# Moving the steps of a time-mixing stage: next scan ahead of the quotient, and a new order for the last of eight batches

## What is computed

```
x = x + _L1_attn_ref(_layernorm(x), ...)          # time mixing, this stage
x = x + _L1_ffn_ref(_layernorm(x), ...)           # its router logits are made in this stage too

k, v = xk @ Wk.T, xv @ Wv.T ; r = sigmoid(xr @ Wr.T)
step: qt = max(pp, kt + u); e1 = exp(pp - qt); e2 = exp(kt + u - qt)
      out = (e1 * aa + e2 * vt) / (e1 * bb + e2)
      pp_new = max(pp + neg_ew, kt); f1 = exp(pp - pp_new); f2 = exp(kt - pp_new)
      aa, bb = f1 * aa + f2 * vt, f1 * bb + f2
ln = layernorm(wkv) * ln_g + ln_b ; result = (r * ln) @ Wo.T
```

## Time and profile before

| What | us |
|---|---|
| median of 3 executions | 732.92 (732.75 to 733.7) |
| the profiled execution, its own time | 731.65 |
| its span in the profile | 729.7 |
| busy in the span: PE / DVE / ACT / POOL | 660.3 / 518.9 / 349.0 / 337.1 |
| the stage of the change: first load of its products to its last matmul | 403 to 564 |

### The profile page before, as it was taken

How to read it: one execution, slowest core, us unless ns; L and a number is a source line. 1 busy time by engine, 2 the same in 40 slices (tenths; PEclk the granted TensorE clock), 3 DMA queues, 4 the chain that set the end, 5 groups by cost and what they waited for, 6 DMA issues and landing times. The chain is left out here.

```text
span 729.7 us, 13761 instructions
## 1 busy us (share of the span) xinstructions
PE 660.3 (90%) x4339; PEld 538.6 (74%) x4339; DVE 518.9 (71%) x1087; ACT 349.0 (48%) x735; POOL 337.1 (46%) x326
## 2 busy tenths in 40 slices
PE   8989999879989999999997999999988679999950
PEld 6656666568868888888886888888877348888840
DVE  5878888957865555544444699998782868888847
ACT  1767777736403333333333565554552844554420
POOL 4977767510053344334224255555331066777530
PEclk9999999998999999999999999999976799999985
DMA  6900000101013111111106940000010022333229
GB/s 197 337 2 3 1 2 15 45 11 53 1 56 105 58 59 51 52 58 55 34 22 206 363 146 2 1 0 1 30 58 30 1 65 76 101 101 102 78 81 311
DMA packets 37185, 54.23 MB, mean 74 GB/s; under 512 B 6644, under 2 KB 28918, under 8 KB 36982
## 3 DMA queue, kind: packets, MB, share of 16 engines
q1 hardware_dynamic: 27832, 31.78, 13.0%
q0 software_dynamic: 7104, 19.41, 8.5%
q10 hardware_dynamic: 2176, 2.10, 0.9%
HBM read 37.28 MB, written 15.99 MB: 73 GB/s over the span
## 5 line engine op out<-in xcount | busy, mean ns | idle before, releaser
L1926 PE MATMUL banks<-r_xt,r_w_mixed 128*128 128x256 f32 x384 | 84.9, 380 | 0.7 <-ACT r_xt L2023 0.7
L1577 DVE SCALAR_TENSOR_TENSOR f0x_s<-f0x_th,banks 128x512 f32<-128x512 f32 x35 | 24.1, 687 | 83.2 <-ACT f0x_th L1536 83.2
L1437 POOL DMA_INDIRECT f_y<-f0x_yout,f_slot_of x35 | 34.5, 984 | 99.6 <-ACT f0x_yout L1552 99.6
L1926 PEld LDWEIGHTS banks<-r_xt,r_w_mixed 128*128 128x128 f32 x384 | 72.1, 189 | 11.0 <-ACT r_xt L2023 1.0
L1536 ACT ACTIVATE f0x_th<-banks 128x512 f32<-128x512 f32 x35 | 21.0, 600 | 86.9 <-PE banks L1488 86.9
L1423 POOL DMA_INDIRECT f0x_xg<-f_xn,f_token_of x35 | 34.9, 996 | 55.7 <-DVE f_slot_of L1046 44.3
L659 DVE TENSOR_REDUCE a_ssum<-a_e 128x6 f32<-128x1536 f32 x32 | 56.0, 1748 | 1.3 <-ACT a_e L526 1.0
L1488 PE MATMUL banks<-f_w_hi,f0x_xt_hi 128*128 x140 | 55.4, 396 | 0.9 <-DVE f0x_xt_lo L1571 0.9
L1488 PE MATMUL banks<-f_w_lo,f0x_xt_hi 128*128 x140 | 55.6, 397 | 0.0
L1423 POOL DMA_INDIRECT f1x_xg<-f_xn,f_token_of x39 | 40.6, 1041 | 32.4 <-DVE f_slot_of L1046 19.3
L1488 PE MATMUL banks<-f_w_hi,f0x_xt_lo 128*128 x140 | 55.2, 394 | 0.0
(11 more groups left out here) (368 smaller groups left out, 1895.9 us busy)
## 6 DMA issues: line engine op xcount, KB each, us to landing
f_w_lo<-in_f_w13T SPq DMA_DIRECT2D x4, 2048.0 KB, 11.1
r_y<-f_y SPq DMA_DIRECT2D x16, 256.0 KB, 4.9
f_w_lo<-in_f_w2T SPq DMA_DIRECT2D x4, 512.0 KB, 15.1
f_xn<-f_rows_normed SPq DMA_DIRECT2D x8, 256.0 KB, 2.1
f_b<-in_f_b SPq DMA_DIRECT2D x1, 2048.0 KB, 10.1
f_w_lo<-in_f_w2T SPq DMA_DIRECT2D x2, 1024.0 KB, 11.9
f_xn<-r_y SPq DMA_DIRECT2D x8, 256.0 KB
f1c_y<-f_y SPq DMA_DIRECT2D x8, 256.0 KB, 7.8
```

Of the source, the lines that this page charges most:

```text
L1437: pool.indirect_dma_start(k.y_dram, bass.IndirectOffsetOnAxis(ap=k.slot_of[:, done:done + 1], axis=0), yout[:, done % YB, :], None).then_i ...
L1577: dve.scalar_tensor_tensor(out=s1[:, t % 2, :], in0=th[:, t % 2, :], scalar=1.0, in1=glu_part, op0=ALU.add, op1=ALU.mult).then_inc(s1_done, 1)
L1926: last = pe.matmul(bank(1 + kind)[:, eb * T:(eb + 1) * T], r.w_mixed[:, kind, j // KB, j % KB, eb * P:(eb + 1) * P], xt[:, b % 2, j % KB, ...
```

## The change

In the loop, `tops(b)` no longer stands in iteration b ahead of `gate(b-1)`, but in iteration b-1, behind the reciprocal and ahead of the multiplication into `r_wkv`, which is now a step of its own (`quotient`). `falls(b)` moves ahead of `gate(b-1)`. `divide` as a step of POOL is unchanged.

After the loop, `shift(7)` moves from behind `centre(7)` to between the router chunks, two matmuls on unused data are added on PE (`keep_clock(2)`, four records), `late_turn(4)` and `late_turn(5)` go between centre and project, `deviate(7)` moves ahead of `project(7)`, and on ACT `late_norm(5)` goes behind `late_turn(3)` and `late_norm(6)` further back.

```
         w.stats(2)
         for z in range(LATE):
             w.shared_add(z)
-        IN_GAP = 4
         for b in range(B):
             if b + 1 < B:
                 front(b + 1)
             if b > 0:
                 w.centre(b - 1)
-            w.tops(b)
+            if b == 0:
+                w.tops(b)
+            w.falls(b)
             if b > 0:
                 w.square(b - 1)
                 w.gate(b - 1)
                 w.shift(b - 1)
-            w.falls(b)
             w.grow(b)
             w.gap(b)
             w.clamp(b)
@@ -1797,6 +1797,9 @@
             if b > 0:
                 w.vary(b - 1)
             w.divide(b)
+            if b + 1 < B:
+                w.tops(b + 1)
+            w.quotient(b)
             if b + 3 < B:
                 w.gather_up(b + 3)
             if b > 0:
@@ -1804,27 +1807,39 @@
             if B - 3 <= b < B - 1:
                 w.late_norm(2 * (b - B + 3))
                 w.late_norm(2 * (b - B + 3) + 1)
+        last = B - 1
         w.late_turn(0)
-        for c in range(IN_GAP):
-            if c + 1 < IN_GAP:
-                w.late_turn(c + 1)
-            if c < 2:
-                w.late_norm(4 + c)
-            w.late_gates(c)
-        w.level(B - 2)
-        for step in (w.centre, w.square, w.gate, w.shift, w.add_shift, w.project, w.deviate, w.vary):
-            step(B - 1)
-        w.late_norm(B - 2)
-        w.late_turn(IN_GAP)
-        for c in range(IN_GAP, B - 1):
-            if c + 1 < B - 1:
-                w.late_turn(c + 1)
-            w.late_gates(c)
-        w.add(B - 1)
-        w.level(B - 1)
-        w.late_norm(B - 1)
-        w.late_turn(B - 1)
-        w.late_gates(B - 1)
+        w.late_turn(1)
+        w.late_gates(0)
+        w.late_turn(2)
+        w.late_norm(4)
+        w.late_gates(1)
+        w.late_turn(3)
+        w.shift(last)
+        w.late_gates(2)
+        w.late_gates(3)
+        w.late_norm(5)
+        w.keep_clock(2)
+        w.centre(last)
+        w.level(last - 1)
+        w.square(last)
+        w.late_turn(4)
+        w.gate(last)
+        w.deviate(last)
+        w.late_turn(5)
+        w.project(last)
+        w.add_shift(last)
+        w.vary(last)
+        w.late_gates(4)
+        w.late_norm(6)
+        w.late_gates(5)
+        w.late_turn(6)
+        w.late_gates(6)
+        w.add(last)
+        w.level(last)
+        w.late_norm(last)
+        w.late_turn(last)
+        w.late_gates(last)
 
     class Work:
         def shared_up(self, z): pass
@@ -1847,6 +1862,8 @@
         def clamp(self, b): pass
         def scan(self, b): pass
         def divide(self, b): pass
+        def quotient(self, b): pass
+        def keep_clock(self, times): pass
         def centre(self, b): pass
         def square(self, b): pass
         def gate(self, b): pass
@@ -1966,6 +1983,11 @@
                                          start=(eb == 0), stop=(eb == EB - 1))
                 last.then_inc(done["var_done"], 1)
 
+            def keep_clock(self, times):
+                pe.wait_ge(done["ku_ready"], B)
+                for _ in range(times):
+                    pe.matmul(bank(1)[:, 0:D], r.cen_other[:], r.w_mixed[:, 0, 0, 0, :], start=True, stop=True)
+
             def late_turn(self, c):
                 pe.wait_ge(done["late_xn"], c + 1)
                 if c == 0:
@@ -2167,7 +2189,10 @@
                 dve.wait_ge(done["ex_done"], b + 1)
                 then(dve.tensor_tensor(den[:], ex[:, 0], ab[:, 1, :, 0:T], ALU.mult), "e1b_done")
                 then(dve.tensor_tensor(den[:], den[:], ex[:, 1], ALU.add), "den_done")
-                then(dve.reciprocal(rden[:], den[:]), "rden_done")
+                dve.reciprocal(rden[:], den[:]).then_inc(done["rden_done"], 1)
+
+            def quotient(self, b):
+                dve.wait_ge(done["rden_done"], b + 1)
                 dve.wait_ge(done["num_done"], b + 1)
                 at_least(dve, done["centred"], b)
                 dve.tensor_tensor(wkv[:], num[:], rden[:], ALU.mult).then_inc(done["wkv_done"], 1)
```

## The result

The changed kernel takes **726.07 us** (median of 4, 724.25 to 727.55) against 732.84 for the kernel before, timed beside it (731.37 to 733.7): ratio 0.9908, 95% interval 0.9888 to 0.9927. That is 6.8 us less; 4.0 had been forecast, and 726.07 lies under the range's lower end, 727.0. The same kernel, run once more among the experiments (`again`), gave 725.94.

What follows compares the result with a forecast made beforehand. In the loop PE is nearly full but DVE sets the later pace; behind it the last quotient, then one chain in line. Last gates 4.0 us sooner, the loop's 0.3 loss included: 732.92 - 4.0 = 728.9 us, range 727.0 to 732.6.

Steps and rivals of the forecast that it cites:

- Part 1: Loop, tops ahead of the quotient and falls ahead of the gate: 0.3 us slower, bounds 1.0 slower to 1.2 faster.
- hand-over: Loop, POOL to DVE: about 0.1 to 0.2 us gained in each of four or five iterations, 0.6 us in all.
- Part 3: PE until the last centre: shift at 1.2 GHz from 540.0 to 543.6, centre ends at 548.15 us against 550.32.
- The collision of the scans with POOL: Loop: moved scans do not run freely beside POOL's addition; they end up behind r_num or push it back.
- the first iteration's loss: Loop's first iteration: the scans come between r_num and r_wkv, for which PE's centre waits, 0.85 to 1.1 us later.
- Part 2: Last batch: exponential 1.9 us sooner, last quotient done at 544.6 instead of 546.49, or 544.9 with the loop's 0.3.
- Rival B: Loop: the scans find room beside POOL and waits for r_rw go, 1.2 to 2 us more gained, 727.2; chance 0.10.
- rival D: Around the shift: the clock never falls, centre 1.2 us sooner than in the forecast's sum, 727.6; chance 0.15.
- Part 4: Last centre to last gates: add at 552.05 instead of 555.63, last gates end at 560.15 instead of 564.18.
- Behind the barrier nothing changes: Phase after the stage, from the barrier to the end: no change in time, 0 us.
- Rival A: Shift through centre: clock stays low, shift and added matmuls delay the last centre, 1.9 us slower, 734.8; chance 0.15.
- Rival C: From the project's end: clock low, PE holds the last turn until 559.0, taking 2.5 of the 4.0, 731.4; chance 0.15.

Runs made afterwards that it cites:

- falls_back: The change with falls(b) behind gate(b-1) again: 733.29 us, ratio 1.0017 to the kernel before.
- tops_behind_quotient: The change with the scans of tops(b+1) behind the quotient of b, falls still ahead of the gate: 725.79 us, ratio 0.9913 to the kernel before.
- tail_only: The kernel before with its old loop and the change's new order after the loop: 728.28 us, ratio 0.9942 to the kernel before.
- shift_back: The change with shift(7) directly behind the last centre again: 729.86 us, ratio 0.9963 to the kernel before.
- loop_only: The kernel before with the change's new loop and the old order behind it: 731.22 us, ratio 0.9988 to the kernel before.
- norm_twice: The change with two unused ACT copies of x_res added ahead of the last late_norm: 726.53 us, ratio 0.9931 to the kernel before.
- first_quotient_first: The change, but in the first iteration the quotient stands ahead of the next scans: 727.27 us, ratio 0.9949 to the kernel before.
- keep_more: The change with keep_clock(2) added behind late_turn(6) and keep_clock(1) behind the last turn: 725.68 us, ratio 0.9919 to the kernel before.
- no_keep: The change without the two added matmuls: 726.82 us, ratio 0.9928 to the kernel before.

## Why the prediction was wrong

The direction and the mechanisms of Parts 2 and 4 were right; the size was not: 6.8 us for 4.0. Part 1's hand-over failed as a mechanism, the shift in Part 3 as a size. Taken together their 0.8 and 1.1 us put the forecast at 727.0; the 0.9 us that are left lie behind the barrier or in the spread of the executions. By its steps:

- **Part 1, tops and falls in the loop: sign wrong, -0.3 for +0.3, 0.8 us in all with the part of it that lies ahead of the loop (0.1).** The collision of the scans with POOL was right (1.68 us for two in place of 1.26, and in `falls_back` 2.23), and the first iteration's loss was nearly right (0.80, forecast 0.85 to 1.1; centre at 427.06, forecast 427.2). The step that failed is "What is left is the hand-over from POOL to DVE, about 0.1 to 0.2 us in each of four or five iterations". It treated only the tops. The falls ahead of the gate bring `r_less`, the exponential, POOL's product with v and the scans of `r_ab` forward in every iteration, and with them `r_num` by 1.30 us; Part 2 counted just this for the last iteration and forgot it for the others. So the scans collide with `r_num` at a time when there is 1.3 us to spare, `r_rw` comes 0.41 sooner, and PE is the bound again at 16.89. `falls_back` shows it by taking it away (17.43), `tops_behind_quotient` by keeping it alone (17.12, same median). The 0.5 us gained lie inside the bounds given for this sum (1.0 slower to 1.2 faster); the value was taken near the wrong one. Rival B's spacing came, though not its reason: the scans did not run freely.
- **Part 2, the last quotient: right.** Exponential at 531.98, quotient done at 544.17; 25.79 us behind batch 7's products, where the forecast's times make 25.74. `falls_back` gives back 2.1 of it.
- **Part 3, PE until the last centre: the term that was mis-sized.** "I take the lower level for the shift" put 3.6 us; it took 1.73 from start to start (539.55 to 541.28), 1.9 less. PE was through with the two added matmuls at 544.10, just ahead of the quotient (544.17), so the centre became the quotient's again and ended at 546.22: 27.83 us behind batch 7's products in place of 28.99, 1.2 us sooner. That is rival D, price and place. The forecast took the time at which the clock fell before, 539.9, over to a stretch that is no longer the same. Before, PE waited 1.13 us there; now 0.25, because the exponentials come sooner. Where that wait comes back, so does the forecast: in `falls_back` and in the profile of `tail_only` PE waits 1.12 us, the clock falls 0.6 and 2.0 us behind that wait, and the shift, which comes only after the fall, takes 3.2 and 2.8 us from start to start. Where the shift is taken out instead (`shift_back`, `loop_only`) the wait is 0.25 as in the change, and the clock falls 3.1 and 3.3 us behind the start of the first gates. In the change the shift begins 2.7 us behind it. So both moves together keep the clock up in these profiles, and each alone does not; that the length of the wait is what counts, and not the moment at which the gates start, was not taken apart.
- **Part 4, centre to the end: right.** Centre's end to add 4.01 us (forecast 3.9), add to the norm's end 4.39 (4.39), last turn to last gates 3.69 (3.65). `norm_twice` confirms that all of it is in line.
- **"Behind the barrier nothing changes": wrong by 1.3 us in the first profile, by 0.5 in that of `again`.** No instruction changed there, but in four of the eighteen profiles, the change's two among them, the clock does not fall at the router's list. What decides it was not found: it is not PE's wait there, and the place of the clock's last rise goes with it without having been tested. How often it happens in executions without a profile is open too, so how much of the median's 6.8 it makes cannot be said. Against the change's first profile, it is also where the gains of `first_quotient_first` (0.7) and `keep_more` (1.3) were lost.

Rival A did not come for the change, but its mechanism is real: in two of six executions of `no_keep` the time is 4 us and more over the change's, and in the profiled one of the two the clock is low through centre and project. The price A was given against the forecast, 5.9 us, fits the 5.8 between the means of the short and the long ones of those six. Rival C did not come: gates 4 and 5 ran at the higher level, 1.85 us for the two, and gates 6 ended at 554.31, 0.31 ahead of the norm. The clock is low for the last turn and the last gates (from 553.8), which costs 1.3 us by `keep_more`, but that was in the forecast's own sum. The transposes around the centre did not bring the clock down: it is 1.00 with eight of them between 546.0 and 548.5 in the change and between 545.6 and 548.1 in `keep_more`, as between 150.5 and 154.5 us before.

## What to carry to other kernels

When an instruction moves ahead on one engine, follow its whole chain through the other engines in every iteration in which it moves, before asking what collides with it; a collision that stands in a row of the trace costs nothing if the same edit has moved the other party away. The time at which the clock fell is a result of the old order and not a property of the place: ask what TensorE will be doing there afterwards, and take both levels into the range. And a gain of a microsecond at one stage's end can be taken back by the clock in the next, as in two profiles here. So judge a version by several executions beside the old kernel on the same chip, ask whether the profiled one was a typical one, and read its profile for where the clock falls.

## What was not expected of the hardware

- The clock can fall with TensorE busy throughout: in `shift_back` it was busy for all of 540 to 545 us, first with turns and matmuls of 8 columns alone, and went from 1.00 to 0.50 just ahead of 542. In the change, with eight records of 256-column matmuls of the shift in the same stretch, it stayed.
- A wait of about 1.1 us can come with a fall, or not: in the profile of `no_keep` the clock fell to 0.50 within the wait of 1.11 us. In the changed kernel PE waits 1.21 us, and the clock stays at 1.00 through it and on to 600 us:

```profile
584.40 1.10 PE L1302 MATMUL banks<-f_w_lo,ident 128*128 128x512 f32 x2 [1.21 <-ACT f_w_lo L1326]
```

- VectorE's scan beside a GpSimd addition takes 1.68 us for two if it starts 0.72 us behind the addition, and then the addition keeps its 1.27; started 0.04 us behind it (`falls_back`), the two scans take 2.23 and the addition 1.73. A GpSimd addition of `x_res` in the change's first iteration took 2.19 us, where 1.27 is usual: it started at 427.87, 0.16 behind VectorE's `r_less`, which ran to 428.93. The prediction's rule from the Trainium skill (SBUF — State Buffer, Who interferes with whom) fits the first case: the scan issued second was held and the addition was not. It fits the third as well, where the addition came second and was the longer by about as much as `r_less` still had to run. In the second case both were longer, which it does not tell.
